# Normalising and transposing the next batch's input earlier in a two-layer decoder kernel

## The reference

```python
x = x + L0_attn(layernorm(x))                 # causal, features from cosines and sines
x = x + L0_xattn(layernorm(x), ctx, mask)     # cross attention, 8 heads, 64 keys
x = x + L0_ffn(layernorm(x))                  # one of 8 experts per sequence
x = x + L1_attn(layernorm(x))                 # causal, 16 heads
x = x + L1_xattn(layernorm(x), ctx)           # cross attention, 16 heads, 64 keys
x = x + L1_ffn(layernorm(x))                  # quantised gate, up and down products
```

## Time and profile before

| | |
|---|---|
| median of three timed runs | 3018.79 us (3016.57 to 3022.42) |
| the profiled execution's own time | 3010.78 us |
| its span, first to last instruction | 3008.8 us |
| mean granted clock of TensorE | 0.867 |
| TensorE busy | 2276.8 us (76%) |
| VectorE busy | 2175.1 us (72%) |
| ScalarE busy | 1060.2 us (35%) |
| GpSimd busy | 585.9 us (19%) |

### The profile page before, as it was taken

How to read it: one execution, slowest core, us unless ns; L and a number is a source line. 1 busy time by engine, 2 the same in 40 slices (tenths; PEclk the granted TensorE clock), 3 DMA queues, 4 the chain that set the end, 5 groups by cost and what they waited for, 6 DMA issues and landing times.

```text
span 3008.8 us, 50636 instructions
## 1 busy us (share of the span) xinstructions
PE 2276.8 (76%) x17470; PEld 1830.6 (61%) x17470; DVE 2175.1 (72%) x4246; ACT 1060.2 (35%) x2004; POOL 585.9 (19%) x666
## 2 busy tenths in 40 slices
PE   3667788868776877886877687888677777888875
PEld 3556666657465756664755565666565566666663
DVE  6765788866866578885776667888586666788767
ACT  2312444422432244442242224444224223444324
POOL 2111222212101122221101112222120102222220
PEclk8778899989777889998877789999877878999988
DMA  6001689840001078983000119897100014899600
GB/s 234 1 15 40 137 160 171 154 86 1 1 15 56 15 149 161 170 152 63 1 1 15 56 37 167 166 164 144 31 1 15 1 55 85 161 169 166 113 1 14
DMA packets 658407, 251.39 MB, mean 84 GB/s; under 512 B 613082, under 2 KB 633946, under 8 KB 657370
## 3 DMA queue, kind: packets, MB, share of 16 engines
q1 hardware_dynamic: 653978, 243.79, 41.4%
q10 hardware_dynamic: 4160, 4.19, 0.4%
HBM read 52.87 MB, written 10.49 MB: 21 GB/s over the span
## 4 chain that ended last, share of the span: by engine, by line
issue 38%; PE 23%; DVE 18%; DMA 11%; ACT 5%; POOL 4%; DVEq 1%; ACTq 0%; SPq 0%; POOLq 0%
DMA l_ptb<-l_phb 6%; PE ps L233 5%; PE ps L235 5%; PE ps L234 4%; DMA l_pts<-l_phs 4%; DVE nmax L1385 3%; PE ps L1289 1%; DVE l_k L1440 1%; DVE l_q L1444 1%; DVE l_phb L1391 1%; DVE l_phs L1391 1%; ACT l_q L1351 1%; PE ps L1271 1%; ACT xn L1347 1%; POOL d_pn L990 1%
## 5 line engine op out<-in xcount | busy, mean ns | idle before, releaser
L1385 DVE TENSOR_REDUCE nmax<-ps 128x1 f32<-128x1024 f32 (+7 forms) x512 | 383.3, 750 | 23.0 <-PE ps L1273 20.9
L1494 POOL CAST l_phb<-l_pb 128x1024 f16<-128x1024 f32 (+3 forms) x256 | 241.4, 943 | 654.1 <-ACT l_pb L1336 337.8
L1336 ACT ACTIVATE l_pb<-ps,nmax 128x1024 f32<-128x1024 f32 (+3 forms) x256 | 244.7, 956 | 283.5 <-DVE nmax L1385 282.7
L1271 PE MATMUL ps<-l_k,l_q 128*128 128x512 f32 (+3 forms) x768 | 319.1, 416 | 24.3 <-ACT l_ps L1336 23.9
L1391 DVE TENSOR_TENSOR l_phb<-l_pb,l_phb 128x1024 f16<-128x1024 f32 (+3 forms) x256 | 288.2, 1126 | 15.5 <-POOL l_phb L1494 13.4
L1272 PE MATMUL ps<-l_k,l_q 128*128 128x512 f32 (+3 forms) x768 | 270.1, 363 | 0.0
L1289 PE MATMUL ps<-l_v,l_ptb 128*128 128x64 f16 x4992 | 197.8, 197 | 34.2 <-DMA l_ptb<-l_phb 34.1
L1289 PEld LDWEIGHTS ps<-l_v,l_ptb 128*128 128x128 f16 x4992 | 177.1, 101 | 67.4 <-DMA l_ptb<-l_phb 41.1
L233 PE MATMUL ps<-xTh,l_w 128*128 128x512 f32 x256 | 123.1, 481 | 83.9 <-DVE l_q L1444 50.5
L1494 POOL CAST l_phs<-l_ps 128x128 f16<-128x128 f32 (+3 forms) x256 | 124.2, 485 | 319.1 <-DMA l_pts<-l_phs 169.6
L1271 PEld LDWEIGHTS ps<-l_k,l_q 128*128 128x128 f32 x768 | 156.0, 203 | 44.2 <-ACT l_ps L1336 29.8
(11 more groups left out here) (361 smaller groups left out, 6279.4 us busy)
## 6 DMA issues: line engine op xcount, KB each, us to landing
l_k<-xn SPq DMA_DIRECT2D x128, 256.0 KB, 4.1
l_w<-l_wqk_s SPq DMA_DIRECT2D x32, 512.0 KB, 4.8
l_wv<-l_wv_s SPq DMA_DIRECT2D x16, 512.0 KB, 6.0
xin<-in_x SPq DMA_DIRECT2D x4, 1024.0 KB, 5.5
m_w<-in_m_w SPq DMA_DIRECT2D x8, 512.0 KB, 4.4
m_w<-in_m_w SPq DMA_DIRECT2D x4, 1024.0 KB, 9.2
l_wo<-in_l_wo SPq DMA_DIRECT2D x16, 256.0 KB, 4.5
l_ptb<-l_phb SPq DMA_TRANSPOSE x256, 4.1
```

The lines of the kernel that those rows point to most:

```text
L1271: pe.matmul(s[:, c0:c1], q, L["l_k1"][:, h, c0:c1], start=True, stop=False)
L1336: s.activation(l_numer(k)[:, 0:n], l_banks(k)[:, 0:n], ACT.Exp, bias=nmax[:, k % 4:k % 4 + 1], accum_out=lsum[:, h, k % NT:k % NT + 1]).th ...
L1385: v.tensor_reduce(nmax[:, k % 4:k % 4 + 1], l_banks(k)[:, 0:n], AX.X, ALU.max, negate=True).then_inc(q_["max"], 1)
L1494: g.tensor_copy(l_parts(k)[:, 0:cols], l_numer(k)[:, 0:cols]).then_inc(q_["hi"], 1)
```

## The change

The norm of batch b + 1's input moves from the start of the last feed-forward stage into the second cross attention of batch b, in seven pieces (`f_v_norm`), one behind each of the first seven tiles of `x_v`. It writes tensors of its own (`n_xn` and the small ones), which lie where the feed-forward stage later keeps `g_h` and `g_r`, and counts on a semaphore of its own, `s_x0`; GpSimd's bias add waits for that one. The four groups are transposed (`f_pe_turn`), copied (`f_a_upper`) and subtracted (`f_v_lower`) around the first two tiles' products, ahead of the loop over tiles, in four banks (4 to 7) in place of two. The steps that follow get new numbers: shell projection 0 (was 2), its normalisation 1, omega product 2, angles and first values 3, sines 4, combinations 4 to 6, second values 6, VectorE's combinations 6 and 7; only the cross attention's product, the feature transposes and their halves are left behind the last add. In the first batch the same functions run one after another, with the old tensors.

```diff
+        def f_v_norm(v, b, k, w):
+            if k < 4:
+                if k == 0:
+                    v.wait_ge(s_xin, b * 16 + 16)
+                for t in (2 * k, 2 * k + 1):
+                    v.bn_stats(w["n_st"][:, t, :], xin[:, t, :])
+            elif k == 4:
+                v.drain()
+                for t in range(NT):
+                    v.bn_aggr(w["n_ag"][:, t, :], w["n_st"][:, t, :])
+                v.drain()
+                v.tensor_scalar(w["n_nv"][:], w["n_ag"][:, :, 1], EPS, None, ALU.add)
+                rsqrt(v, w["n_rsd"][:], w["n_nv"][:])
+            else:
+                for t in range(4 * (k - 5), 4 * (k - 5) + 4):
+                    v.tensor_scalar(w["n_xn"][:, t, :], xin[:, t, :], ..., ALU.subtract, ALU.mult).then_inc(s_x0, 1)
+        def f_bank(g):
+            return 4 + g
...
         def x_v(v, cr, b, more=False):
...
                 if t + 2 < NT:
                     sum_(t + 2)
+                if more and t < 7:
+                    f_v_norm(v, b + 1, t, N)
...
         def f_g(g, b):
             x_diagonal_first(g, b)
-            g.wait_ge(s_xn, b * (NPH * NT) + NT)
+            g.wait_ge(s_x0, b * NT + NT)
...
         def g_pe(pe, b, more):
             turn_x(0)
+            if more:
+                f_pe_turn(pe, b + 1, 0, N)
+                f_pe_turn(pe, b + 1, 1, N)
             pe.wait_ge(g_sem["xT"], b * 2 + 1)
...
             updown(0)
             turn_x(1)
+            if more:
+                f_pe_turn(pe, b + 1, 2, N)
             updown(1)
             pe.wait_ge(g_sem["xT"], b * 2 + 2)
+            if more:
+                f_pe_turn(pe, b + 1, 3, N)
+                pe.wait_ge(s_lo, b * (NTR * NG) + NTR * NG + 2)
...
         def g_v(v, b, more):
             if more:
-                f_v(v, b + 1, 0)
+                for g in range(2):
+                    f_v_lower(v, b + 1, g)
             hidden(0)
+            if more:
+                for g in range(2, NG):
+                    f_v_lower(v, b + 1, g)
...
         def g_a(s, b, more):
             copy_x(0)
+            if more:
+                for g in range(2):
+                    f_a_upper(s, b + 1, g)
             silu(0)
             copy_x(1)
+            if more:
+                f_a_upper(s, b + 1, 2)
             silu(1)
+            if more:
+                f_a_upper(s, b + 1, 3)
...
         def f_pe(pe, b, t):
+            elif t in (4, 5):
+                for u in (2 * t - 8, 2 * t - 7):
+                    pe.wait_ge(a_sem["ph"], b * 2 + 1)
...
+                    f_pe_comb(pe, u)
             elif t == 6:
                 pe.wait_ge(C0.s["kvT"], b * 2 + 2)
+                pe.wait_ge(a_sem["ph"], b * 2 + 2)
+                for u in range(4, NT):
+                    if u < 6:
+                        pe.wait_ge(a_sem["ya"], b * NT + u - 1)
                     f_pe_comb(pe, u)
                 for g in (2, 3):
-                    pe.wait_ge(a_sem["ya"], b * NT + g + 1)
                     f_pe_value(pe, b, g)
+            elif t == 7:
                 x_pe_m(pe, C0, b)
...
         def comb_bank(u):
-            return (0, 1, 2, 3, 6, 7, 0, 1)[u]
+            return (6, 7, 6, 7, 6, 7, 0, 1)[u]
```

More of the change, by code:

```diff
@@ L285, in ln_step, with f_pe_turn, f_turned, f_a_upper @@
                                 ALU.subtract, ALU.mult).then_inc(s_xn, 1)
-        def ln_v(v, b, n, src):
-            for k in range(NT):
-                ln_step(v, b, n, src, k)
+        N0 = {"n_xn": xn, "n_st": st, "n_ag": ag, "n_nv": nv, "n_rsd": rsd}
+        def f_v_norm(v, b, k, w):
[13 more added lines that the diff above has]
+                for t in range(4 * (k - 5), 4 * (k - 5) + 4):
+                    v.tensor_scalar(w["n_xn"][:, t, :], xin[:, t, :], w["n_ag"][:, t, 0:1], w["n_rsd"][:, t:t + 1],
+                                    ALU.subtract, ALU.mult).then_inc(s_x0, 1)
+        def f_bank(g):
+            return 4 + g
+        def f_pe_turn(pe, b, g, w):
+            pe.wait_ge(s_x0, b * NT + 4 * (g // 2) + 4)
+            for c in range(DC):
+                for t in range(2):
+                    o = ps[:, f_bank(g), c * 256 + t * P:c * 256 + (t + 1) * P]
+                    last = pe.transpose(o, w["n_xn"][:, 2 * g + t, c * P:(c + 1) * P], idf[:])
+            last.then_inc(s_tr, 1)
+        def f_turned(g):
+            return ps[:, f_bank(g), :].rearrange("p (c t) -> p c t", c=DC), slice(2 * g * P, (2 * g + 2) * P)
+        def f_a_upper(s, b, g):
+            bank, cols = f_turned(g)
+            s.wait_ge(s_tr, b * (NTR * NG) + g + 1)
+            s.copy(xTh[:, :, cols], bank).then_inc(s_hi, 1)
+        def f_v_lower(v, b, g):
+            bank, cols = f_turned(g)
+            v.wait_ge(s_hi, b * (NTR * NG) + g + 1)
+            v.tensor_tensor(xTl[:, :, cols], bank, f32(xTh[:, :, cols]), ALU.subtract).then_inc(s_lo, 1)
         NTR = NPH - 1
@@ L633, in f_v @@
         def f_v(v, b, t):
[L635 to L639 removed]
+            if t == 1:
                 for g in range(2):
@@ L1935, in v_rest @@
             ln_lo(v, b, 4)
-            x_v(v, C1, b)
+            x_v(v, C1, b, more)
             g_v(v, b, more)
@@ L1996, in _ @@
             s.wait_ge(s_sv, SV)
+            for g in range(NG):
+                f_a_upper(s, 0, g)
             for t in range(NT + 1):
-                if t == 6:
+                if t == 4:
                     s.wait_ge(s_ws, 64)
@@ L2011, in _ @@
             setup_split_v(v)
+            for k in range(7):
+                f_v_norm(v, 0, k, N0)
+            for g in range(NG):
+                f_v_lower(v, 0, g)
             for t in range(NT + 1):
@@ L2025, in _ @@
             x_pe_kv(pe, C0, 0)
+            for g in range(NG):
+                f_pe_turn(pe, 0, g, N0)
             for t in range(NT + 1):
```

79 lines of the change are left out of this document (34 added, 45 removed).

## The result

The changed kernel took 3033.17 us (median of 11 runs, 3024.21 to 3041.45) against 3016.57 us for the kernel before, timed beside it (11 runs, 3004.11 to 3026.79): a ratio of 1.0060, 95% interval 1.0038 to 1.0081, so 18 us more (11.5 to 24.4). The forecast was +3 with a range of 3002 to 3038, and the time lies inside the range, near its upper end. It was not the likeliest case that came, but the slower rival, the clock at the tail, in two of the three places, together with a part A above its bound. The profiled execution took 3035.12 us, with a span of 3033.2 and a mean granted clock of 0.861.

What follows compares the result with a forecast made beforehand. No engine's busy total bounds the kernel; VectorE and TensorE wait for each other by turns. Terms +7.0, -2.4, -8.0, +4.4 make +1.0 us a batch, +3 in three: 3013.8 profiled, 3021.8 timed; range 3002 to 3038.

Steps and rivals of the forecast that it cites:

- the likeliest case: Forecast case, chance 0.40: gains and losses between batches nearly cancel, +1.0 us a batch, +3 in three.
- the slower rival, the clock at the tail: TensorE at clock 0.50 when the feed-forward tail's bundle starts: +6.6 us a batch, +20, 3039 us; chance 0.20.
- part A: Norm placed in the second cross attention delays its last add: +7.0 us a batch, between +4.6 and +8.
- the first piece of 0.7: Norm piece after tile 0 in the cross attention: fits a VectorE wait, costed at nothing; first four up to 2.8 uncovered.
- The 4.0 piece: Norm piece after tile 4 in the cross attention: does not fit a wait; GpSimd's product adds at most 1.1 us.
- the first 1.3 piece: Norm piece after tile 5 in the cross attention: 1.3 us, plus up to 1.6 waiting for GpSimd's product.
- B: Feed-forward start, quantised input to second hidden tile: -2.4 us a batch despite GpSimd's add blocking VectorE; bounds -4.6, -1.7.
- the rival in which blocks don't bite: GpSimd operations do not hold up VectorE's: -3.5 us a batch, -10.5 in all, 3008 us; chance 0.30.
- C: Second hidden tile to the sine's low half: -8.0 us a batch; -7.4 at the low clock, -9.9 at the high.
- D: Sine's low half to first attention tile: two tiles still to come, +4.4 us a batch, between +3.4 and +9.4.
- The sum: Between batches: A +7.0, B -2.4, C -8.0, D +4.4 give +1.0 us a batch, +3 in three; nothing gained.
- One of the prediction's own signs of being wrong: Wrong if the feed-forward stage, 99.8 us before, shrinks by clearly more or less than 6 us.

Runs made afterwards that it cites:

- Three: Changed kernel with three norm pieces (aggregates and root, two of scalings) moved later, where VectorE had waited; 3014.96 us, ratio 0.9987 to the kernel before.
- six: Changed kernel with norm statistics before the cross attention's first maximum, root behind tile 1's low half, scalings at tile 7; 2998.19 us, ratio 0.9937.
- one: Changed kernel with GpSimd's bias add held back until the first hidden tile in batches 1 to 3; 3015.44 us, ratio 0.9986.
- eight: Kernel before, with an extra unread GpSimd add right behind the diagonals; 3029.15 us, ratio 1.0037.
- Seven: Changed kernel with GpSimd's add held back, norm pieces in early gaps and at tile 7, tile 6's down product before the bundle; 2998.87 us, ratio 0.9951.
- nine: Changed kernel with GpSimd's add held back and norm statistics and root early, scalings at tile 7; 2998.69 us, ratio 0.9938.
- five: Changed kernel with eight unread 512-column matmuls ahead of tile 6's transposes, in a TensorE wait; 3021.03 us, ratio 1.0020.
- eleven: Changed kernel with late GpSimd add, norm pieces in gaps, down product before the bundle, six unread matmuls before the shell projection; 2973.53 us, ratio 0.9853.
- ten: Changed kernel with late GpSimd add, early norm pieces, and unread matmuls: six ahead of tile 0's transposes, eight ahead of tile 6's; 2982.3 us, ratio 0.9884.

## Why the prediction was off, point by point

**What bounds it.** Right: neither engine's total told anything; the differences that the rows explain are waits of one engine for another, or the clock.

**A, the first step that failed: a term undersized, +10.1 for +7.0 (bound 8).** By VectorE's landmarks inside the stage (first place), the sums of tile 6, ahead of which only the small pieces lie, are already 1.5 us late. The first transposes ran at the low clock (1.97 us instead of 1.32), which is 0.65 and no piece's doing (0.2 in the third place); the first piece of 0.7, costed at nothing, puts off the low half behind it by 0.6; the other three cost nothing. Another 0.3 is a short idle stretch of VectorE inside the running norm for which the trace names no wait. The 4.0 piece with its block then gives 4.9, the first 1.3 piece with its block 2.9, which is what the prediction had for them (4.0 + 1.1, 1.3 + 1.6); but the prediction let 0.7 of it be absorbed by later waits, and nothing was. The last 0.8 are TensorE's: having stood for 8.64 us, its products ran at 0.73. Three and six show that this is the place, not the work.

**B, right: -2.0 for -2.4.** The block came with its predicted length, on the other half of the quantisation, and the rival in which blocks don't bite (0.30) is refuted by one and eight. The prediction left open which of two ready instructions goes first. In the rows GpSimd's add begins at 769.68, while the third of VectorE's four like operations runs unhindered to 769.87; the fourth then waits for the whole add. The evidence that the prediction drew on was read a little wide: the 1.47 us of the earlier trace rows at 2230.41 are four operations, and only the last of them, 2231.48 to 2231.88, is beside the VectorE operation of 2231.58; and the rule made of it, that an operation from on-chip to on-chip memory waits, does not hold for the aggregates at 736.89.

**C, right in its mechanism, larger: -9.9 on average for -8.0.** The prediction chose a value near the low clock's end, because TensorE idles half of the time ahead of the projection. The projection still began at the full clock and lost it half way (0.75). For the projection at the full clock it had -9.9. Seven and nine show the case that it had taken, at 0.50; which of the two comes was not to be read from the trace of before.

**D, the step that turned the result: +8.8 on average for +4.4.** The prediction took 1.0 of the up to 6.0 us that the low clock costs behind tile 6's hidden product, reasoning that the bundle is dense and the clock had risen within such a run before. In the first and the third place it did not rise before the bundle's end, 8.8 us at 0.50, and D was +9.4 and +11.4; the latter is over the bound of 9.4, since the kernel before had its shortest D there. In the second place the bundle ran at 1.00 and D was +5.5, near the forecast. The sum also took the product of queries and keys at the full clock (3.1 us to the low half), and it was 4.2 to 4.9 in the three places, at 0.50 to 0.62. The rival had exactly the first case, with +9.4 for D, and gave it 0.20. It had C at -7.4 in the same case and so +20 in all; here the full clock came at C and the low one at D, and A made up the difference.

**The sum.** With the measured terms it is +10.1 - 2.0 - 9.9 + 8.8 = +7.0 a batch, 21 in three; the timed ratio gives 18. That the sooner start pays little, since two tile steps now follow the chain's end, was right, but the tail grew by almost what C had saved only with the low clock's help. The range held partly by luck: A was 2 us a batch over its bound, and C, at the far end of its own, paid for that. One of the prediction's own signs of being wrong did come: the feed-forward stage shrank by 2.2, 5.8 and 1.4 us in the three places, not by some 6 in each.

## What to carry to other kernels

Work moved from one stage into another costs what it delays the other engine there, not its busy time: the same 9.35 us of VectorE made the stage 10.1, 4.0 or 1.2 us longer by their place (means of the three places: as changed, in three, in six), so look for the waits of the engine and put the pieces into those, away from GpSimd's operations. Where GpSimd becomes free to start sooner, ask which on-chip VectorE operation it will shut out. And before a long run of small matmuls, look at the granted clock at its start, in every repetition and not in one: a few unread matmuls in the wait ahead of it took between 12 us (five) and 30 us (eleven against seven) off here.

## What the runs showed of the hardware

A VectorE operation of four elements a partition lasted 4.07 us beside a GpSimd add, where it takes 0.17 alone (eight); one of a single element beside the same kind of add kept its 0.15 us (one), and eight aggregates beside a GpSimd product their 0.64 (the changed kernel). What sets them apart, the runs don't show.

TensorE can be busy without a gap for 10.3 us and stay at the low clock throughout (nine, 48 matmuls of 66 columns, 0.50); in ten the same matmuls began at the full clock and lost it in the middle (0.71) with no idle time. So being busy without a gap did not keep the clock here, let alone raise it. The two kernels differ by the unread matmuls alone, so what ran ahead of them decided it here.

Ten's unread matmuls take TensorE 3.4 us a batch (1.46 for the six, 1.89 for the eight) and made the kernel 16 us faster, since they stood in waits.

The head of the first batch, to its first attention tile, took between 118.1 and 122.1 us in these kernels, though its code was the same in all the changed ones; a difference of 1 or 2 us in one trace is no evidence.
